# Attention phase of a Macaron block: the once-per-sequence job on TensorE moved from the end of a step to behind the next step's scores

## The reference, cut to what matters

```python
x = x + attn(layernorm(x))            # B, T, C = 16, 256, 128; H = 16 heads of D = 8
qkv = x @ W_attn + b_attn             # q, k, v
att = einsum('bhtd,bhsd->bhts', q, k) / sqrt(D) + rel_bias
att = softmax(where(causal, att, -inf))
y = einsum('bhts,bhsd->bhtd', att, v)
return y @ W_proj + b_proj
```

## Time and profile before

| | |
|---|---|
| time, median of 3 runs | 1420.02 us (1418.97 to 1423.3) |
| span of the profiled execution, first to last instruction | 1415.3 us |
| PE busy | 1301.7 us, 92% |
| DVE, ACT, POOL busy | 958.2 us, 783.4 us, 780.1 us |
| steps of the attention phase (first scores to last scores) | 75.2 to 373.1 us of the span |

### The profile page before, as it was taken

How to read it: one execution, slowest core, us unless ns; L and a number is a source line. 1 busy time by engine, 2 the same in 40 slices (tenths; PEclk the granted TensorE clock), 3 DMA queues, 4 the chain that set the end, 5 groups by cost and what they waited for, 6 DMA issues and landing times. The chain is left out here.

```text
span 1415.3 us, 35725 instructions
## 1 busy us (share of the span) xinstructions
PE 1301.7 (92%) x10556; PEld 1109.4 (78%) x10556; DVE 958.2 (68%) x4074; ACT 783.4 (55%) x1882; POOL 780.1 (55%) x1027
## 2 busy tenths in 40 slices
PE   6789999999786788999978999999999979999998
PEld 5567777777575577888867999999888867888887
DVE  5557676767486774556545787888878858566564
ACT  2257777777625533444424766676667654444443
POOL 2167777777434174555533556566577663344453
PEclk9989999999976999999988999999999999999999
DMA  5199930000033011221112122122122102222221
GB/s 154 41 273 272 271 97 0 0 0 1 6 105 108 12 66 34 29 31 29 29 22 52 50 50 53 45 52 50 48 57 60 42 27 71 51 29 30 30 30 15
DMA packets 102600, 85.67 MB, mean 61 GB/s; under 512 B 10504, under 2 KB 90090, under 8 KB 102203
## 3 DMA queue, kind: packets, MB, share of 16 engines
q1 hardware_dynamic: 83796, 65.90, 16.9%
q0 software_dynamic: 17280, 16.17, 6.5%
q10 hardware_dynamic: 1382, 1.83, 0.5%
HBM read 21.32 MB, written 45.78 MB: 47 GB/s over the span
## 5 line engine op out<-in xcount | busy, mean ns | idle before, releaser
L1909 POOL TENSOR_TENSOR attn_z<-attn_top,attn_z 128x256 f32<-128x256 f32 x256 | 155.9, 618 | 60.1 <-DVE attn_top L1856 60.1
L1856 DVE CUSTOM_DVE_ANT_0 attn_z<-banks,rel_bias 128x128 f32<-128x128 f32 (+1 forms) x512 | 148.5, 353 | 42.1 <-PE banks L2004 40.6
L2386 POOL TENSOR_TENSOR ret_rotated<-ret_twins 128x512 f32<-128x512 f32 x64 | 82.1, 1284 | 134.3 <-DVE ret_twins L2296 134.1
L1942 ACT ACTIVATE attn_prob<-banks 128x384 f32<-128x384 f32 x256 | 119.2, 492 | 7.2 <-PE banks L2014 2.4
L930 DVE SCALAR_TENSOR_TENSOR moe_block_act<-banks,moe_block_weights,moe_block_gated 128x128 f32<-128x128 f32 x276 | 77.7, 344 | 64.2 <-ACT moe_block_gated L985 39.4
L2449 ACT ACTIVATE ret_normed<-banks,ret_head_shift,ret_head_rstd 128x128 f32<-128x128 f32 x256 | 96.5, 459 | 44.0 <-DVE ret_head_shift L2320 43.5
L1475 DVE SCALAR_TENSOR_TENSOR moe_block_act<-banks,moe_block_weights,moe_block_gated 128x128 f32<-128x128 f32 x276 | 77.7, 344 | 62.9 <-ACT moe_block_gated L1569 38.9
L2014 PE MATMUL banks<-ident,attn_z 128*128 128x128 f32 x768 | 109.0, 278 | 0.7 <-ACT attn_prob L1942 0.7
L2014 PEld LDWEIGHTS banks<-ident,attn_z 128*128 128x128 f32 x768 | 84.4, 141 | 14.4 <-issue 14.1
L2481 PE MATMUL banks<-ret_x_hi,ret_hi 128*128 128x256 f32 x256 | 85.1, 332 | 1.9 <-ACT ret_gate L2442 1.0
L1522 POOL DMA_INDIRECT out<-moe_block_y,moe_taken x37 | 58.5, 1581 | 47.8 <-ACT moe_block_y L1579 39.7
(11 more groups left out here) (367 smaller groups left out, 4248.6 us busy)
## 6 DMA issues: line engine op xcount, KB each, us to landing
slots<-moe_pad SPq DMA_DIRECT2D x12, 2560.0 KB, 23.4
ret_twins<-ret_twins SPq DMA_DIRECT2D x256, 64.0 KB, 2.0
moe_stage<-in_moe_w SPq DMA_DIRECT2D x4, 576.0 KB, 5.9
bias_reversed<-scratch SPq DMA_DIRECT2D x1, 2048.0 KB, 9.0
y_rows<-moe_pad SPq DMA_DIRECT2D x1, 2048.0 KB, 8.8
back_of_seq<-y_rows SPq DMA_DIRECT2D x16, 128.0 KB, 2.3
out<-x_res SPq DMA_DIRECT2D x8, 256.0 KB, 2.4
ret_stage<-in_ret_w SPq DMA_DIRECT2D x16, 96.0 KB, 2.1
```

Source lines behind the costliest of these rows:

```text
L1856: last = dve.tensor_tensor_reduce(out=z[:, s, cols], in0=ps_s[:, i, cols], in1=bias, scale=1.0, scalar=-3.0e38, op0=ALU.add, op1=ALU.max, ...
L1909: pool.tensor_tensor(z[:, s, P:WIDTH], top[:, s, 1:2].to_broadcast([P, WIDTH - P]), z[:, s, P:WIDTH], ALU.subtract).then_inc(shifted1, 1)
L1942: act.activation(prob[:, slot(k, i), :], ps_p[:, i % 2, 0:WIDTH], ACT.Exp, scale=-1.0).then_inc(prob_ready, 1)
L2386: pool.tensor_tensor(rotated[:, k % 2], twins[:, k % 2, 0], twins[:, k % 2, 1], ALU.add).then_inc(rotated_ready, 1)
```

## The change

The four jobs move in PE's list from behind `transpose_heads` to directly behind `scores`, with leads one smaller. The sequence of PE's operations is the same but for this: what stood just ahead of a step's scores now stands just behind them. PE's largest lead is 8 instead of 9, and so one iteration is unrolled at its end and not two. On DVE `residual` and `add_v_bias` move from ahead of `bias_and_max` of head 0 to behind it (`layernorm` stays ahead of it); on ACT `copy_xT` and `copy_yT` move from ahead of the `shift_tile0` of head 2 to behind it. No operation, buffer or wait is added or removed.

```diff
             software_pipeline(dve, BATCHES // GU, U, [
-                (2, divide), (0, per_seq(LAST, residual)), (10, per_seq(0, layernorm)), (7, per_seq(0, add_v_bias)),
-                (5, of_head(0, bias_and_max)), (9, per_seq(0, normalise)), (5, of_head(1, bias_and_max)),
-                (5, of_head(2, bias_and_max)), (5, of_head(3, bias_and_max))])
+                (2, divide), (10, per_seq(0, layernorm)), (5, of_head(0, bias_and_max)),
+                (0, per_seq(LAST, residual)), (7, per_seq(0, add_v_bias)), (9, per_seq(0, normalise)),
+                (5, of_head(1, bias_and_max)), (5, of_head(2, bias_and_max)), (5, of_head(3, bias_and_max))])
...
             software_pipeline(act, BATCHES // GU, U, [
-                (3, of_head(3, exponent)), (8, per_seq(0, copy_xT)), (1, per_seq(LAST, copy_yT)), (4, of_head(2, shift_tile0)),
+                (3, of_head(3, exponent)), (4, of_head(2, shift_tile0)), (8, per_seq(0, copy_xT)), (1, per_seq(LAST, copy_yT)),
                 (3, copy_avT), (4, of_head(0, exponent)), (4, of_head(1, exponent)), (6, copy_qk), (4, of_head(2, exponent)),
                 (5, of_head(0, shift_tile0))])
...
             software_pipeline(pe, BATCHES // GU, U, [
-                (5, scores), (3, attend), (4, of_head(0, transpose_z)), (4, of_head(1, transpose_z)), (6, project_qk),
-                (4, of_head(2, transpose_z)), (4, of_head(3, transpose_z)), (3, transpose_heads),
-                (1, per_seq(LAST, project_out)), (2, per_seq(LAST, transpose_y)), (9, per_seq(0, transpose_x)), (8, per_seq(0, project_v))])
+                (5, scores), (0, per_seq(LAST, project_out)), (1, per_seq(LAST, transpose_y)), (8, per_seq(0, transpose_x)), (7, per_seq(0, project_v)),
+                (3, attend), (4, of_head(0, transpose_z)), (4, of_head(1, transpose_z)), (6, project_qk),
+                (4, of_head(2, transpose_z)), (4, of_head(3, transpose_z)), (3, transpose_heads)])
```

## The result

The changed kernel takes 1428.93 us (median of 12 runs, 1425.4 to 1436.46), the kernel before 1418.93 us in 12 runs beside it (1416.06 to 1433.37). The ratio is 1.0064, with a 95% interval of 1.0038 to 1.0089: slower, by 9 us (10.0 us between the medians). The forecast was +6.6 us, 1426.6 us. The profiled execution spans 1426.0 us against 1415.3, and 10.1 us of the 10.7 between them lie between the first and the last scores of the attention phase: 75.30 to 383.12 us of the span, where it was 75.16 to 372.86. The rest is in the last sequence's tail; what follows the phase's last instruction takes 1028.5 us against 1029.1.

A forecast was written before the change was run, and what follows sets the result against it. TensorE's order of work was taken to set the attention phase's time. Terms 6.8 + 0.8 + 0.5 - 1.0 - 0.5 = +6.6 us, added to 1420.0, gave 1426.6 us; range 1420 to 1433 us.

The forecast's parts named there:

- Nothing gained by the move: PE's step: scores wait for ACT's copy of q and k as the job did, so steps stay as long as before.
- The write of y: Steps with `transpose_y`: attend waits for DVE's `divide` writing `y`, 0.45 us of idle PE in 15 sequences, +6.8 us.
- DVE behind it: DVE's work queued later: no stall after the write, but steps with `project_out` lengthen by 0.05 us, 15 times, +0.8 us.
- The start: Phase start: the first moved `transpose_x`, formerly hidden by the scores' wait for DVE, costs about +0.5 us at half clock.
- Loop ends: Ends of PE's loop iterations: the branch falls into the wait for the copy, five times 0.2 us, -1.0 us.
- Unrolled steps: PE's unrolled last iterations: one of two enters the loop, saving under 0.1 us in each of eight steps, -0.5 us.
- rival 2: DVE becomes the bound: its two late steps end 0.2 us later, scores wait 6 us more, 1433 us; chance 0.12.
- the one for `y`: Sign in the profile: attend's loads idle about 0.8 us behind `transpose_y`'s, 15 times, in steps of 5.0 us, not 4.53.
- rival 3: Scores behind transposes: the extra change of tiling is exposed, 0.17 us 60 times, +10 us, 1437 us; chance 0.05.
- the cheap switch out of the scores (1): Scores to full-array job takes 0.80 us, not 0.87: -4.2 us, 1422.4 us, chance 0.18; strong form 1413 us, chance 0.05.
- That attend does not wait for the write (4): Attend after `transpose_y`: no wait for the write of `y`, 0 instead of 6.8 us, total 1420 us; chance 0.02.

The follow-up runs named there:

- e1: Changed kernel with two copies of `y`, so `divide` no longer waits for `transpose_y`: 300.1 us from first to last scores, ratio to the kernel before 1.0013.
- e5: Changed kernel with the old order on DVE and ACT, only PE's jobs moved: 313.1 us from first to last scores, ratio to the kernel before 1.0068.
- e2: Changed kernel with the two waits of `scores` swapped, DVE's before the copy's: 304.4 us from first to last scores, ratio to the kernel before 1.0034.
- e3: Changed kernel with two copies of `y` and the waits of `scores` swapped: 296.4 us from first to last scores, ratio to the kernel before 0.9961.
- e9: Changed kernel with two copies of `y` and swapped `scores` waits, run again in another sitting: 296.8 us from first to last scores, ratio 0.9985.
- e6: Kernel before with only the two waits of `scores` swapped: 297.1 us from first to last scores, ratio to the kernel before 0.9963.
- e10: Changed kernel with two copies of `y` and the waits of `scores` and `copy_qk` swapped: 295.5 us from first to last scores, ratio 0.9958.
- e11: Kernel before with only the two waits of `copy_qk` on ACT swapped: 296.0 us from first to last scores, ratio to the kernel before 0.9941.
- e4: Kernel before with only the edits on DVE and ACT, PE's jobs still ahead of the scores: 300.4 us from first to last scores, ratio 1.0006.

## Why the prediction was right, and where it was off

The sign and the range held, and so did the mechanism that the forecast rests on, the wait on `y`. But one term of 4.5 us, some 40% of the change, was missing. By its own terms, in the profile:

- **Nothing gained by the move: right, but not "as long as before".** Step for step PE waits for the copy as before, and then loses 0.08 us more (below, "Missed"). The choice between 0.80 us (half of the 1.60 us that the earlier trace rows has at a granted clock of 0.50) and 0.87 us for scores to job fell on the right one: 0.87 in each step, and no run shows 0.80. The job costs its 0.37 or 0.64 us behind the scores as ahead of them (attend at 1.24 and 1.51).
- **The write of y: right, +6.8 forecast, +7.7 measured.** Attend's first matmul stands at 1.71 us in six steps and 1.78 in nine, where e1 has 1.24: 6 x 0.47 + 9 x 0.54 = 7.7. What was mis-sized is the last leg, from the write's end to attend's load, 0.12 us and not 0.06: in the row it was taken from the earlier trace rows the load itself carries the wait for `y`, here a plain wait operation ahead of it does. e1 shortens each of these steps by 0.48 or 0.55 us; of its 7.7 us from scores to scores, 7.2 are these steps, of which that stretch has 14, and 0.4 lie in the first five steps.
- **DVE behind it: +0.8 forecast, nothing measured.** No step with `project_out` is longer than its job makes it. The step that failed is the latency of 0.14 us from DVE's last read to the scores, taken from one row at the phase's start; e5 shows 0.05 us. The row is at a granted clock of 0.50 and in unrolled code, where DVE's wait stands as a plain operation of 0.05 us ahead of the load; in e5 the load carries it. In the changed kernel DVE is done at 4.58 or 4.71 us against scores at 4.89. In e2, where the steps are shorter, it is this near: scores 0.12 us late in one step of eight.
- **The start: +0.5 forecast, not to be told.** The first five steps take 24.20 us for 24.22, but two profiles of one kernel (e3, e9) differ by 0.47 us there.
- **Loop ends: -1.0, right.** The steps behind a loop's end show no extra 0.2 us. **Unrolled steps: -0.5, right** within 0.1: eight of PE's steps that were unrolled are in the loop now (48 before, 56 after).
- **Missed: +4.5 us,** 56 steps of 0.08. The text said that the scores stand 0.04 us behind the copy and that the trace has this case. It has it only in unrolled steps, where the scores' load carries the wait for the copy. In the loop an arithmetic operation ahead of the load carries it; the job used to meet that wait first, and now nothing does. The forecast put this at nothing by assuming that a wait costs the same wherever it stands. e2 and e6 show that it does not.

By this account 7.7 + 4.5 - 1.0 - 0.5 is 10.7 us; from the first scores to the phase's last instruction the profile has 11.1, so 0.4 us are not accounted for.

The three latencies that were off (0.04, 0.06 and 0.14 us) have this in common: each was read from a row where the late wait stood on another kind of operation than in the place it was used for, on the load or ahead of it. And there is some luck in the total. Without the missed term the account is 6.2 us, near the forecast's 6.6, because two terms that did not come (0.8 and 0.5) nearly make up for the y wait being 0.9 us longer. The missed term then fitted into a range that was drawn for other reasons, rival 2 and the spread of the runs. e2, the changed kernel without its loop part, has a ratio whose interval includes 1 (0.9995 to 1.0072): that the change is clear of the noise may be partly owed to what the forecast did not have.

Of its own signs, the one for `y` held with other sizes (loads idle 0.69 us, steps of 5.16 us), and two failed: the steps with `transpose_x` and `project_v` should have been as long as before and are 0.08 us longer, and the scores' loads idle 0.37 us and not 0.3. All kinds of step longer is the sign of rival 3, at half its size; e2 decides between them.

On the rivals: the cheap switch out of the scores (1) is excluded by 0.87 us in each step. VectorE as the bound (2) is near but absent. That attend does not wait for the write (4) is excluded by e1. On the exposed change of tiling (3): scores, attend and the rest of PE's work differ in the tile of the array that they load (in the profile 32*128, 128*32 and 128*128), and the new order has one change of tile more in a step: heads to scores, scores to job, job to attend, where it was job to scores, scores to attend. In the changed kernel the loads idle 0.33 us from scores to job (to 168.89) and 0.20 from attend to the transposes (to 170.59). From job to attend it is 0.17 us behind two transposes (to 179.30, and in e1), and 0.12 behind the four matmuls of `project_out` (174.05 + 0.52 = 174.57 to 174.69). Between transposes and the heads' transposes, all 128*128, they don't idle (one group's loads end at 176.80 + 0.67 = 177.47, the next begins at 177.44). No run changes a tile alone, so what holds the loads back in these places is not shown. The change from the heads to the scores adds nothing in e2: its 0.29 us are all for the copy, as with a job there.

## What to carry to other kernels

Moving work to another place on the engine that sets the time gains nothing where both neighbours wait for the same thing; then ask what now stands between a producer and its consumer in one step: here a buffer with one copy (`y`) put 0.5 us per sequence on the path. Where an operation waits for two semaphores, find out which of the two the working instruction carries: the late one should be on it (here a start 0.04 to 0.05 us behind the end of what it waits for, against 0.10 to 0.12), and the early one on the operation ahead. In this kernel's loops, where arithmetic for the second value is needed, that means waiting first for the one that comes early; in its unrolled code it was the other way round (e2). So a latency read from a row of unrolled code does not price the same wait in the loop. An order on one engine and the orders on those it works with are one design: of this change the half on DVE and ACT alone costs 2.7 us, the half on PE alone 15.4, and both together 10.1.

## What the runs showed of the hardware that was not expected

- A late wait costs by where it stands. On the working instruction itself, that instruction starts 0.04 to 0.05 us behind the end of what it waits for (scores in unrolled steps, e2's loop, e5; the copy on ACT; the write of `y` on DVE in six sequences). On a plain wait operation ahead of it, 0.10 to 0.12 us (attend's wait for `y`; unrolled scores in e2 0.11; the write of `y` on DVE in nine sequences 0.11; e10's and e11's last copies on ACT 0.10). On an arithmetic operation ahead of it, 0.12 us (the changed kernel's loop; ACT in three steps of eight). These operations last 0.017 to 0.051 us by the profile, less than the 0.06 to 0.08 us that they add.
- The loop steps of the attention phase repeat to 0.01 or 0.02 us over executions, sittings and kernels with the same order, while the program's total spreads by 17 us and more. The first scores came at 75 us in six profiles and at 81, 84 and 92 us in the others, the difference arising in the LoRA block ahead; and the part behind the phase took 1028 to 1032 us in two sittings and 1062 to 1069 in the other two. A change of 2 us in the phase can be read from step lengths when no ratio of totals could tell it.
- In the loop `normalise` took 0.70 us (e1, e4) to 0.94 us (e2) of DVE's time, from its start to that of the next operation, and 0.82 in the kernel before (0.91 once). What made the difference wasn't tried.
